# Theta and phi through the stage buffer, four copies a half, a second part for copied tiles, and units in new slots

## The reference

```python
t, p = W_theta @ x + b_theta, W_phi @ x + b_phi        # 64 x 1024 each
f = softmax(t.T @ p / 8)                               # 1024 x 1024
x = x + W_fuse @ (x @ f.T) + b_fuse
h = group_norm(x)                                      # 32 groups
q, k, v = q_w @ h + q_b, k_w @ h + k_b, v_w @ h + v_b  # 128 x 1024 each
x = x + p_w @ (v @ softmax(q.T @ k / sqrt(128)).T) + p_b
```

## Time and profile before

| | us |
|---|---|
| median of 3 runs (lowest to highest) | 1897.72 (1893.85 to 1898.34) |
| the profiled execution, its own time | 1896.21 |
| its span, first to last instruction | 1894.4 |

### The profile page before, as it was taken

How to read it: one execution, slowest core, us unless ns; L and a number is a source line. 1 busy time by engine, 2 the same in 40 slices (tenths; PEclk the granted TensorE clock), 3 DMA queues, 4 the chain that set the end, 5 groups by cost and what they waited for, 6 DMA issues and landing times.

```text
span 1894.4 us, 34418 instructions
## 1 busy us (share of the span) xinstructions
PE 1715.3 (91%) x8970; PEld 1103.0 (58%) x8970; DVE 1445.5 (76%) x1669; ACT 1445.6 (76%) x2152; POOL 1260.9 (67%) x1321
## 2 busy tenths in 40 slices
PE   3799999999999999999999999999999999999986
PEld 2455565656566665556665566665656565556553
DVE  4577778788778777778787778788778877878754
ACT  3587778778778777878787878777878777878754
POOL 2467766667776667776666776666776666776653
PEclk9799999999999999999999999999999999999999
DMA  2587787877787777878877878877878777778764
GB/s 53 115 141 149 158 169 148 160 157 151 162 164 159 158 159 147 164 155 161 161 155 148 165 154 163 165 147 156 164 150 166 162 146 160 163 147 166 149 134 95
DMA packets 860086, 286.33 MB, mean 151 GB/s; under 512 B 822305, under 2 KB 823201, under 8 KB 860065
## 3 DMA queue, kind: packets, MB, share of 16 engines
q1 hardware_dynamic: 860064, 286.08, 74.8%
HBM read 50.86 MB, written 17.04 MB: 36 GB/s over the span
## 4 chain that ended last, share of the span: by engine, by line
issue 25%; DVE 17%; ACT 14%; DMA 13%; PE 11%; POOL 10%; SPq 7%; DVEq 1%; POOLq 0%; ACTq 0%
DMA et<-pair 9%; SPq L350 6%; DVE neg_max L723 6%; PE o_ps L426 6%; ACT s_ps L622 4%; DMA rden_dram<-rden 3%; ACT pair L647 3%; PE s_ps L426 3%; DVE pair L740 2%; DVE phi L814 2%; PE s_ps L464 2%; POOL y_sb L974 2%; DVE x L777 2%; DVE x_max L800 2%; ACT et L632 2%
## 5 line engine op out<-in xcount | busy, mean ns | idle before, releaser
L426 PE MATMUL o_ps<-et,v_hi 128*128 128x512 f16 x2048 | 696.9, 382 | 39.9 <-DVE x L777 27.3
L723 DVE TENSOR_REDUCE neg_max<-s_ps 128x1 f32<-128x1024 f32 x512 | 624.5, 1220 | 62.7 <-PE s_ps L426 52.2
L740 DVE SCALAR_TENSOR_TENSOR pair<-s_ps,pair 128x1024 f16<-128x1024 f32 x256 | 312.3, 1220 | 105.6 <-ACT pair L647 104.6
L426 PE MATMUL o_ps<-et,v_lo 128*128 128x512 f16 x1024 | 390.0, 381 | 0.0
L426 PEld LDWEIGHTS o_ps<-et,v_hi 128*128 128x128 f16 x2048 | 202.7, 99 | 283.6 <-issue 92.5
L426 PE MATMUL s_ps<-phi,theta 128*128 128x512 f32 x1024 | 330.8, 446 | 9.2 <-ACT e_copied L622 4.5
L622 ACT ACTIVATE s_ps<-s_ps,neg_max 128x1024 f32<-128x1024 f32 x256 | 277.2, 1083 | 60.4 <-DVE neg_max L723 59.7
L875 POOL TENSOR_TENSOR pair<-e_copied,pair 128x1024 f16<-128x1024 f32 x128 | 274.2, 2142 | 27.5 <-ACT pair L645 27.5
L964 POOL TENSOR_TENSOR x<-x,xr 128x512 f32<-128x512 f32 x64 | 81.1, 1267 | 283.4 <-DVE x L777 283.4
L734 DVE SCALAR_TENSOR_TENSOR et<-s_ps,et 128x1024 f16<-128x1024 f32 x128 | 156.7, 1224 | 146.4 <-ACT et L632 146.4
L647 ACT ACTIVATE pair<-s_ps 128x1024 f16<-128x1024 f32 x256 | 261.9, 1023 | 8.1
(11 more groups left out here) (131 smaller groups left out, 2885.1 us busy)
## 6 DMA issues: line engine op xcount, KB each, us to landing
rden_row<-rden_dram SPq DMA_DIRECT2D x128, 256.0 KB, 3.8
xs<-in_x SPq DMA_DIRECT2D x32, 512.0 KB, 3.9
phi<-phi SPq DMA_DIRECT2D x64, 256.0 KB, 3.1
out_y<-y_sb SPq DMA_DIRECT2D x64, 256.0 KB, 2.4
et<-pair SPq DMA_TRANSPOSE x384, 4.6
rden_dram<-rden SPq DMA_DIRECT2D x128, 2.0 KB, 1.5
w_f<-in_w_fuse_t SPq DMA_DIRECT2D x1, 64.0 KB, 2.2
ident_sb<-in_ident SPq DMA_DIRECT2D x1, 64.0 KB, 2.1
```

The lines of the kernel that those rows point to most:

```text
L426: mm = pe.matmul(out, lhs_t, rhs, start=start and n == 0, stop=stop and n == len(terms) - 1)
L723: nc.vector.tensor_reduce(neg_max[:, t % 4:t % 4 + 1], s_ps[:, part(t), :], AX.X, ALU.max, negate=True).then_inc(s_max, 1)
L740: nc.vector.scalar_tensor_tensor(out=pair[:, r, 1, :], in0=s_ps[:, part(t), :], scalar=E_SCALE, in1=pair[:, r, 0, :], op0=ALU.mult, op1=AL ...
```

## The change

Theta and phi become staged units: ACT writes all 128 channels to `stage` in one instruction with the bias, POOL makes hi and lo in a new tile `tp_hl` (128 partitions, hi and lo, 512 columns, one tile for each half), and SP copies from there with four transfers a half: phi hi and lo to partitions 0 to 63, the same to 64 to 127, theta hi to 0 to 63, theta lo to 64 to 127. They are issued in slots 12 and 14. DVE has no part in it. `pair` gets a fourth part, which the copied tile of every second group uses. The units get new slots: w0 goes to 7, q1 to 8, mx to 9, w1 to 11, v0 to 14. For k, q and tp units PE does the two products with the hi part of the input first and waits for the lo part only then. The first quarter of a value product waits only for the first half of v or w, the third quarter for the second.

```diff
-PAIRS = 3
+PAIRS = 4
-UNITS = {0: "gn1", 1: "gn2", 2: "v1", 4: "k0", 5: "k1", 6: "q0", 7: "q1", 8: "w0", 9: "w1", 10: "tp0", 12: "tp1",
-         14: "mx", 15: "v0"}
+UNITS = {0: "gn1", 1: "gn2", 2: "v1", 4: "k0", 5: "k1", 6: "q0", 7: "w0", 8: "q1", 9: "mx", 10: "tp0", 11: "w1",
+         12: "tp1", 14: "v0"}
+STAGE = {"v1": 0, "k0": 1, "k1": 0, "q0": 1, "w0": 0, "q1": 1, "tp0": 0, "w1": 1, "tp1": 0, "v0": 1}
+SPLIT_LAG = {"v1": 2, "k0": 1, "k1": 1, "q0": 1, "w0": 1, "q1": 1, "tp0": 1, "w1": 1, "tp1": 1, "v0": 1}
-PHI_SLOTS = {11: "tp0", 13: "tp1"}
+TP_COPY_SLOTS = {12: "tp0", 14: "tp1"}
+TP_COPIES = 4
...
+            def tp_copies(it, s):
...
-                sp.wait_ge(s_tp, before(tp_at, it, unit) + 1)
+                sp.wait_ge(s_split, before(staged_at, it, unit) + 1)
                 sp.sem_inc(s_carrier)
-                sp.dma_start(phi2[0:D, :, cols].bitcast(F32), phi2[D:C, :, cols].bitcast(F32)).then_inc(s_phi, 16)
+                sp.wait_ge(s_scores, before(tile_at, it, PHASE))
+                sp.sem_inc(s_carrier)
+                theta_hl, phi_hl = (tp_hl[half][rows, :, :].bitcast(F32) for rows in (slice(0, D), slice(D, C)))
+                sp.dma_start(phi2[0:D, :, cols].bitcast(F32), phi_hl).then_inc(s_tp_copy[half], 16)
+                sp.dma_start(phi2[D:C, :, cols].bitcast(F32), phi_hl).then_inc(s_tp_copy[half], 16)
+                sp.dma_start(theta2[0:D, cols].bitcast(F32), theta_hl[:, 0, :]).then_inc(s_tp_copy[half], 16)
+                sp.dma_start(theta2[D:C, cols].bitcast(F32), theta_hl[:, 1, :]).then_inc(s_tp_copy[half], 16)
...
# PE, scores
                     if s == 0:
-                        pe.wait_ge(s_phi, 16 * before(tp_at, it, 0))
+                        for n in range(2):
+                            pe.wait_ge(s_tp_copy[n], 16 * TP_COPIES * before(mx_at, it, 0))
...
# PE, unit (k, q and tp)
+                    pe.wait_ge(hi_sem, hi_value)
...
+                        product(m_ps[:, :], [(w[:, 0, :], hi[:, px]), (w[:, 1, :], hi[:, px])], stop=False)
+                        pe.wait_ge(lo_sem, lo_value)
+                        mm = product(m_ps[:, :], [(w[:, 0, :], lo[:, px])], start=False)
...
# ACT, take_unit
-                if name[0] == "t":
-                    cols = slice(int(name[-1]) * HALF, (int(name[-1]) + 1) * HALF)
-                    act.wait_ge(s_scores, before(tile_at, it, PHASE))
-                    nc.scalar.activation(theta2[0:D, cols], m_ps[0:D, :], ACT.Identity,
-                                         bias=vec_ready[0:D, 0:1]).then_inc(s_theta, 1)
-                    nc.scalar.activation(phi2[D:C, 0, cols], m_ps[D:C, :], ACT.Identity,
-                                         bias=vec_ready[D:C, 0:1]).then_inc(s_evac, 1)
-                    return
...
+                elif name[0] == "t":
+                    nc.scalar.activation(to, m_ps[:, :], ACT.Identity, bias=vec_ready[:, 0:1]).then_inc(s_evac, 1)
...
# DVE: the two rests of theta and phi go; the value scale moves behind the reciprocals
-                if here(tp_at, it, s):
-                    dve.wait_ge(s_theta, before(tp_at, it, s) + 1)
-                    nc.vector.scalar_tensor_tensor(out=theta2[D:C, cols], in0=m_ps[0:D, :],
...
# POOL, split_units
+                if name[0] == "t":
+                    pool.wait_ge(s_tp_copy[half], 16 * TP_COPIES * or_none(before(mx_at, it, s) - 1))
+                    hi, lo = tp_hl[half][:, 0, :], tp_hl[half][:, 1, :]
+                    hi_read = hi.bitcast(F32)
```

More of the change, by code:

```diff
@@ L162, in until_part_before, with until_stage_before, last, place @@
         return value(lambda i: count(kind, 0, (part_before(i, s) or 0) + 1), it)
+    def until_stage_before(it, s):
+        def last(i):
+            g = SLOTS * i + s
+            return next((p for p in range(g - 1, -SLOTS - 1, -1)
+                         if staged_at(p) and STAGE[UNITS[p % SLOTS]] == STAGE[UNITS[s]]), -SLOTS - 1)
+        return value(lambda i: count(staged_at, 0, last(i) + 1), it)
+    def place(s):
+        return PAIRS - 1 if s % GROUP == COPIED and s // GROUP % 2 else s % GROUP
     def same_pair(s):
-        return lambda g: int(tile_at(g) and g % GROUP == s % GROUP)
+        return lambda g: int(tile_at(g) and g % GROUP != TURNED and place(g) == place(s))
     def same_group(s):
@@ L220, in attention_pair @@
         phi2 = sb("phi2", [C, 2, N], F32R)
+        tp_hl = [sb(f"tp_hl{n}", [C, 2, HALF], F32R) for n in range(2)]
         q_hi, q_lo = sb("q_hi", [C, N], F32R), sb("q_lo", [C, N], F32R)
@@ L298, in attention_pair @@
         s_den = sem("den_scaled_ready")
-        s_phi = sem("phi_twice")
+        s_tp_copy = [sem(f"theta_phi_copied{n}") for n in range(2)]
         s_split_hi = sem("unit_split_hi")
@@ L445, in scores @@
                     if s == PHASE + GROUP:
-                        pe.wait_ge(s_split, before(staged_at, it, 8))
+                        pe.wait_ge(s_split, before(staged_at, it, 9))
                 out = s_ps[:, part(s), half * HALF:(half + 1) * HALF]
@@ L473, in values @@
                 if quarter == 0:
-                    for r in range(PAIRS):
-                        pe.wait_ge(s_pair_t[r], 16 * before(same_pair(r), it, first + GROUP))
+                    for t in range(first, first + TURNED):
+                        pe.wait_ge(s_pair_t[place(t)], 16 * before(same_pair(t), it, first + GROUP))
                     pe.wait_ge(s_tlo, before(turned_at, it, first + GROUP))
+                    if first % SLOTS == 0:
+                        pe.wait_ge(s_split, before(staged_at, it, first))
+                    if first % SLOTS == PHASE:
+                        pe.wait_ge(s_split, before(staged_at, it, first))
+                    pe.wait_ge(s_taken, before(group_at, it, first))
+                if quarter == 2:
                     if first % SLOTS == 0:
@@ L639, in pair_hi @@
                     return
-                n, r = before(tile_at, it, t), t % GROUP
+                n, r = before(tile_at, it, t), place(t)
                 act.wait_ge(s_exp, n + 1)
@@ L954, in copied_lo @@
                         pool.wait_ge(s_copied_hi, before(copied_at, it, t) + 1)
-                        rest(pair[:, COPIED, 1, :], e_copied[:, :], pair[:, COPIED, 0, :], s_copied)
+                        rest(pair[:, place(t), 1, :], e_copied[:, :], pair[:, place(t), 0, :], s_copied)
             def outputs(it, s):
```

40 lines of the change are left out of this document (14 added, 26 removed).

## The result

The changed kernel takes 1913.40 us (median of 4 runs, 1909.72 to 1917.07) against 1897.79 for the kernel before (median of 4 runs): a ratio of 1.0087, 95% interval 1.0062 to 1.0111. It is slower by 0.9%, where I had forecast 1830 us and 3.5% faster. Its profiled execution took 1909.72 us, with a span of 1907.9 and a mean granted clock of 0.978 (before 0.991).

A forecast was written before the change was run, and what follows sets the result against it. PE was taken as the bound: a floor of 52.15 us a period, plus 1.9 for transposes and copies and 0.3 for ACT and POOL, made 54.35 against 56.5. Over 31 periods, with a longer start: 1830 us, range 1785 to 1880.

The forecast's parts named there:

- The fourth part of `pair`, put at 2.05 us a period: ACT no longer waits at the copied tile; PE's waits before tp0 and q0 go, 1.10 + 0.61 us and two tails.
- POOL's 3.8 us: POOL's added work a period in slots 12 to 14, covered by 8.5 us of idle time and costed at nothing.
- The floor of 52.15: Microseconds a period if PE never waited at four places: 56.5 less 3.50 of waits and 0.85 of hidden drains.
- four take about 2.1 us with gaps: SP's time to issue a half's four copies, against 0.62 us; a theta copy put between 0.3 and 0.62.
- for tp0 they now stand behind tile 10's transpose rather than before it, a gain there: On SP's queue, the first half's copies no longer precede tile 10's transpose; a gain, no size given.
- E: Start of slot 13's last value matmul, 1032.92 in the kernel before; the forecast's times are counted from it.
- ahead of their way back, where SP waits for DRAM anyhow: Slot 14: the second half's copies issue between the reciprocals' write and read-back, while SP waits for DRAM anyhow.
- the copies land about E + 4.7 + 3.1 = E + 7.8: Second half's copies, needed by slot 0's scores at E + 6.7: some 1.1 us of wait at slot 0.
- rival B: Each of tp1's four transfers follows the one before; slot 0 waits 8.4 us, 60.9 a period, about 2030 us; chance 0.08.
- PE's late coming to slot 2 pays for the 0.6 us: Slots 2 to 6: transposes against PE's arrival would cost 0.6 us, but PE's lateness at slot 2 covers it.
- what was put down to ACT and POOL: An allowance of 0.3 us a period for ACT and POOL now being closer to PE.
- C: Copies 3.7 us behind the transposes, PE, ACT, POOL and DMA near full: 56.1 a period, 1885 us; chance 0.15.

The follow-up runs named there:

- single copies: Changed kernel with one transfer of 128 partitions and 512 KB a half in place of four with 768 KB, theta staying zero: 1803.89 us, ratio 0.9490.
- two transfers a period: Changed kernel with two transfers a period for eight, 768 KB for 1.5 MB; ACT writes theta's high part, POOL splits into `phi2`: 1848.87 us, ratio 0.9719.
- eight small: Changed kernel with its four copies a half cut to 64 of 512 columns, an eighth of the bytes: 1860.94 us, ratio 0.9783.

## Why the prediction was wrong

*Right: where the gain is.* The fourth part of `pair`, put at 2.05 us a period (64 us in 31), measured 59 us alone and 40 in the changed kernel. The waits before tp0, before q0 and of slot 14 are gone, and the exponential costs 0.1 us a period instead of 0.88. POOL's 3.8 us are covered by its idle time. The floor of 52.15 was not reached by any kernel, but the one with single copies came to 53.5.

*The step that failed: "four take about 2.1 us with gaps", and that "for tp0 they now stand behind tile 10's transpose rather than before it, a gain there".* The price was taken from a copy that stands alone in SP's queue, with half for theta. The issues took 0.62, 0.61, 0.68 and 1.28 us, 3.3 with gaps. Half the bytes did not make an issue shorter, and the fourth of four took twice as long as the first; with small transfers it did not. And I looked at what the first half's copies do to the transposition ahead of them, not at who stands behind: the reciprocals, ready at E + 1.9, leave at E + 3.3 (mean) instead of my 2.3. That moves all of the second half's copies and the transposes of slots 15 to 1 by 1 us; making the first half's copies small brought 29 us. The same step says of the second half's copies that they stand "ahead of their way back, where SP waits for DRAM anyhow". The wait for DRAM ends too soon for that: the reciprocals had landed at 20.8 us of the period and were read back at 22.8, behind the fourth issue, and the transposes behind them.

*Then "the copies land about E + 4.7 + 3.1 = E + 7.8".* I let the fourth issue begin at E + 4.7 and take the 3.1 us of a copy of phi by itself. It began at E + 5.9 (mean) and took 3.6: E + 9.5 instead of 7.8. From the first of these issues to the fourth it was 2.0 us, as I had it; the 1.2 us of delay came from what stood ahead, the reciprocals and before them the first half's copies. The wait at slot 0 became 3.0 us instead of 1.1. My own sum already had the condition for slower: rival B's landing later than E + 10.7, that is a wait above 4.05 us with nothing else lost. The wait stayed below it, and the rest came from elsewhere.

*That in slots 2 to 6 PE's late coming to slot 2 pays for the 0.6 us.* It did not: slot 6 waits 1.2 us in the changed kernel, and 1.3 in the kernel with single copies, where PE comes to slot 2 early. Another 0.4 us stands at slot 2 and 0.2 before the transposes of slot 4.

*Not in the sum at all: the granted clock.* The wait at slot 0 has a stretch at 0.50 behind it in 13 of 20 periods, 0.8 us a period (the averages of slot 0: scores 0.05, transposes 0.41, value product 0.32 longer). The sum after: 52.15 + 3.0 + 0.8 + 0.4 + 0.2 + 1.2 - 0.5 = 57.2, against 57.1 measured. The 0.5 is taken off because these waits are read from start to start, which makes each 0.35 us longer than its idle time, where the floor counts 0.17 for a drain; there are three a period. Against the forecast's 54.35 that is 1.9 us more at slot 0, 1.2 at slot 6 and 0.8 for the clock, and 1.0 less in the rest: 0.4 at slot 2, 0.1 of what was put down to ACT and POOL, and these 0.5.

*Which rival.* None as written. C ("nearly all comes back") has the right size, 56.1, but by transposes pushed back by bytes; B has the right place, slot 0, but by transfers one after another. They did overlap: the last landed 5.65 us behind the first issue (19.17 to 24.82), not 12.4. What the Trainium skill says on the page "DMA: Bandwidth & Descriptors", in "Rules for kernel authors", to use one transfer of 128 partitions instead of two of halves, the runs bear out in its advice: one transfer in place of four was worth 56 us even against four of an eighth of the bytes each. Its ground, that the halves share the engines, can explain the bytes' part only; the rest began with SP's time, for which I had weighed the rule at nothing.

*What stays open.* No arrangement tried gives the right result near the 1804 us of the single transfer; the best were the fourth part alone, 1844 and 1843, which beat both kernels, and two transfers a period, 1849. The bytes (58 us) and the number of issues (56 us) were told apart only along one path, from eight whole to eight small to two larger transfers, so an interaction between them is in both figures. How much of each came by the clock and how much by the waits wasn't tried by itself either. Why SP takes 1.28 us for the fourth issue is open: whether by its place behind three others or by something in this transfer, no run tells apart.

## What to carry to other kernels

Before a transfer is split in four, count its issues on the queue and write down who stands behind them on that queue: here a tiny write of reciprocals was held up by copies that nobody needed yet, and all transposes came after it. Don't take the price of an issue from one that stands alone: here the fourth in a row took 1.28 us, against 0.62 alone. When several edits come as one change, run each part alone: one part of this change made the kernel 3.1% faster, and the whole was 0.9% slower.

## What I had not expected of the hardware

- The issues of four plain transfers in a row took 0.62, 0.61, 0.68 and 1.28 us on SP, the fourth 0.60 when all are an eighth as large; on ACT, while SP issues transposes, the fourth took up to 2.8 us.
- 512 KB landed 3.2 us after issue on 128 partitions and 4.3 on 64. 256 KB took 2.5 us on 128 partitions (`out_y`, leaving the core) and 3.0 on 64 (theta's low part) in the kernel with two transfers a period. (These are medians; the transfers stand at different places of the period.)
- After 2.9 us without a matmul the granted clock fell to 0.50 for some 3 us (rows above), in a kernel whose PE is 90% busy. That happened in 13 of 20 periods, mostly behind idle times of 2.0 to 3.2 us, and with the second half's copies small in 12 of 20, behind idle times of 1.7 to 2.1 us. In the kernel before, whose longest such wait was 1.4 us, it stood at 1.00 throughout this stretch. So part of a wait's price stands behind it, in matmuls that take longer.
- Two waits of one place can end within 0.3 us of each other (slot 14 with the fourth part alone); the view names only the later, and removing it gains nothing.
